# Keys and values of a second layer made in the experts' stage, and one accumulator for all experts

## The chip, the core and the metric

The kernel runs on one core of one Trainium2 chip, as one program. The core has five engines with a queue each: TensorE (matmuls; PE in the profile), VectorE (DVE), ScalarE (ACT), GpSimd (POOL) and SyncE (SP, which here only starts DMA transfers). They meet in semaphores alone. Sixteen DMA engines move data between DRAM and SBUF, the core's memory of 128 partitions; matmuls write to PSUM, eight banks of 512 f32 per partition. The metric is the device time in microseconds (us).

## The reference

64 sequences (NB) of 128 tokens with 256 features (D) go through two layers. `ctx` is one more input, a context for each sequence, the same in both layers.

```
x = x + tanh(g0) * attention0(layernorm(x), ctx, ctx)      # 16 heads of 16
x = x + tanh(h0) * experts(layernorm(x))                   # 64 experts, 8 for each token, at most 256 tokens each, and a shared one
x = x + tanh(g1) * attention1(layernorm(x), ctx, ctx, mask)
x = x + tanh(h1) * ffn(layernorm(x))                       # inner size 704, weights and activations rounded to 8 bits

attention(q, k, v) = softmax((q @ wq.T + bq) (k @ wk.T + bk).T / 4) (v @ wv.T + bv) @ wo.T + bo
expert e:  y[tokens of e] += gate[token, e] * (silu(x @ w1[e].T) * (x @ w3[e].T)) @ w2[e].T
```

The weights of the 8-bit FFN are scaled by the maximum of each row, rounded, and clipped.

## The kernel before, in words

The program has stages with a barrier of all engines behind each (`phase_end`).

Stage 2 is the first attention. Each engine runs through slots, one a sequence, and a function such as `values(k)` works on the sequence that its lag names (`attention_slots`, `stage(lag)`). A sequence's row of the residual stays in SBUF, in `res[:, b, :]`. At a slot's end `xa`, the residual with the shared expert's part added, is stored to the first accumulator in DRAM and zeros to the second; `token_rows` gets the normalised tokens with their gates. In the stage's last slots and behind them the weights of the 8-bit FFN are quantised: `weights_dve` on VectorE, `weights_pe` transposes, `weights_act` copies, and `ffn_weights_out` stores them to `ffn_int`. SyncE then loads the second layer's attention weights and the weights of the first experts.

Stage 3 is the experts', one slot an expert. GpSimd gathers 2 x 128 token rows two slots ahead (`gather`: two indirect DMAs, `xr<-token_rows`). TensorE transposes them (`rows_t`), multiplies by the first two weights (`up`, matmuls of 256 columns) and by the third (`down`). VectorE makes the hidden values and scales the outputs by the gate (`ye`). GpSimd adds them to an accumulator in DRAM (`add`: two indirect DMAs that accumulate). Expert b goes to accumulator b mod 2, and its add waits for the add of expert b - 2, since two adds at a time to one row would lose one. After the last expert TensorE and ScalarE make the keys and values of three sequences (`first_keys_values_pe`, `first_keys_values_act`).

Stage 4 is the second attention, slots again. SyncE loads the context and a row of both accumulators, VectorE adds the two into `res` (`first_sum`). TensorE, in each slot: `scores(m)` with the mask written first, `project_qk(f)`, `project_v(f)`, `scores_t(k)` with its mask, then transposes, `output`, `maxima_t` and `values`. `scores` and `scores_t` both write all of `tiles`, four banks of PSUM. VectorE's row maximum `mt` (L810) reads what `scores` wrote, and `scores_t`, of the sequence before, waits for it; ScalarE's exponential (L601) reads what `scores_t` wrote, and the next `scores` waits for that. Keys, and queries, are copied out of PSUM with their bias by ScalarE in `copy_qk`, values in `copy_v`.

Stages 5 and 6 are the 8-bit FFN, which the change leaves as it is. The order on each engine is the order in which the code issues; there is no scheduler.

Of the kernel before, what the change touches and what calls it, by code (L numbers as in the profile page):

```python
# [5 lines left out]
def flamingo_gated_two_layers(nc: bass.Bass, a, out: bass.AP):  # L6
# [44 lines left out]
    KV_FIRST = 3  # L51
# [3 lines left out]
    acc = [nc.dram_tensor(f"accumulator_{n}", [T + HALVES * P, D], f32).ap() for n in range(2)]  # L55
# [7 lines left out]
    hidden_away = nc.dram_tensor("hidden_away", [len(AWAY), P, IC * CT], f32).ap()  # L63
    ffn_int = nc.dram_tensor("ffn_int", [3, P, KC * IP], bf16).ap()

    ctx = ExitStack()
    with ctx:
# [146 lines left out]
        wraw = [qkp[:, 3 * n:3 * n + 3, :].rearrange("p a (c d) -> p (a c) d", d=D) for n in range(2)]  # L214
        wdraw = cxax[:, 0:6, :].rearrange("p a d -> p (a d)")[:, 0:KC * I].rearrange("p (k i) -> p k i", k=KC)
        wq_b = pt[1][:, 2:4, :].rearrange("p a d -> p (a d)").bitcast(bf16)[:, 0:KC * IP]
        ws = [w.rearrange("p a d -> p (a d)").bitcast(bf16)[:, 0:KC * IP] for w in (pt[0][:, 2:4, :], ovs[:, :, :], qkp[:, 0:2, :])]
# [78 lines left out]
        MADE_WEIGHTS = (8 if IREST else 6) * 2 + 11  # L296
# [26 lines left out]
        TILES_IN_0 = 8 * NB  # L323
# [3 lines left out]
        def attention_pe(pe, L):  # L327
            def sm(name):
                return f"{name}_{L}"

# [8 lines left out]
            def scores(m):  # L339
# [4 lines left out]
                wait(pe, sm("exp_done"), b - 1)  # L344
# [9 lines left out]
                last.then_inc(sem(sm("s_done")), 1)  # L354

            def scores_t(k):
# [4 lines left out]
                pe.wait_ge(sem(sm("max_done")), ahead(b, 2))  # L361
                if L == 1:
                    masks(1)
                pe.wait_ge(sem(sm("qm_done")), b + 1)
# [6 lines left out]
                last.then_inc(sem(sm("st_done")), 1)  # L371

            def maxima_t(m):
# [4 lines left out]
                pe.wait_ge(sem(sm("max_done")), b + 1)  # L378
# [6 lines left out]
                nc.tensor.transpose(bk[:, 0:P], mt[:, :], ident[:, :]).then_inc(sem(sm("mt_done")), 1)  # L385

            def values(k):
# [5 lines left out]
                pe.wait_ge(sem(sm("exp_done")), b + 1)  # L393
                pe.wait_ge(sem(sm("v_out")), b + 1)
                wait(pe, sm("at_out"), b)
# [5 lines left out]
                last.then_inc(sem(sm("pv_done")), 1)  # L401

            def transposes(f):
# [6 lines left out]
                if L == 0:  # L410
                    pe.wait_ge(sem(sm("v_out")), b + 1)
                else:
                    wait(pe, sm("v_out"), b)
# [4 lines left out]
            def project_qk(f):  # L418
# [5 lines left out]
                pe.wait_ge(sem(f"tile_in{r}"), (2 - L) * (4 * (b - r) + 16) + L * TILES_IN_0)  # L424
# [5 lines left out]
                for j in range(KC):  # L430
                    for n, w in enumerate((w_q, w_k)[:1 if L == 1 and b < KV_FIRST else 2]):
# [4 lines left out]
                last.then_inc(sem(sm("qk_done")), 1)  # L436

            def project_v(f):
                if f is None or (L == 1 and f[0] < KV_FIRST):
                    return  # L440
                b, r = f
                pe.wait_ge(sem(f"tile_in{r}"), (2 - L) * (4 * (b - r) + 16) + L * TILES_IN_0)
                if L == 0:
                    wait(pe, sm("silu_done"), b - 4)
                    wait(pe, sm("qm_done"), b - 1)
                else:
                    pe.wait_ge(sem(sm("xt_out")), b + 1)
# [3 lines left out]
                last.then_inc(sem(sm("v_done")), 1)  # L451

            def output(k):
# [4 lines left out]
                pe.wait_ge(sem(sm("at_out")), b + 1)  # L458
                if L == 0:
                    wait(pe, sm("x2t_out"), b)  # L460
                else:
                    pe.wait_ge(sem(sm("qm_done")), ahead(b, 3))
# [10 lines left out]
            def heads_to_tokens(k):  # L473
# [4 lines left out]
                pe.wait_ge(sem(sm("ov_out")), b + 1)  # L478
                for g in range(NG):
                    last = nc.tensor.transpose(bank[7][:, g * P:(g + 1) * P], ov[r % 2][:, g, :], ident[:, :])  # L480
                last.then_inc(sem(sm("ot_done")), 1)

            def tokens_to_heads(k):
# [4 lines left out]
                pe.wait_ge(sem(sm("on_done")), b + 1)  # L488
                for c in range(KC):
                    last = nc.tensor.transpose(bank[7][:, c * P:(c + 1) * P], on[r % 2][:, c * P:(c + 1) * P], ident[:, :])  # L490
                last.then_inc(sem(sm("at_done")), 1)
# [11 lines left out]
            def moe_up(k):  # L503
# [7 lines left out]
                pe.wait_ge(sem(sm("qm_done")), ahead(b, 4))  # L511
# [46 lines left out]
            def body(stage):  # L558
# [17 lines left out]
                else:  # L576
                    project_qk(f)
                    project_v(f)
# [11 lines left out]
        def attention_act(act, L):  # L590
            def sm(name):
                return f"{name}_{L}"
# [1371 lines left out]
        def _(dve):  # L1964
# [36 lines left out]
            for _ in ffn_weights:  # L2001
                pass
# [63 lines left out]
```

## Time and profile before

| | us |
|---|---|
| median of 3 runs | 2065.47 (2064.66 to 2066.73) |
| the profiled execution | 2067.25 |
| its span in the profile | 2065.4 |
| TensorE busy in the span | 1779.3 (86%) |
| VectorE busy | 1411.1 (68%) |
| ScalarE busy | 1108.9 (54%) |
| GpSimd busy | 562.2 (27%) |

Busy times are sums over stages with different limits, so they name no bound. A row of the timeline or the chain begins with its start in us and its length; `L1438` is line 1438 of the kernel; `accumulator<-ye,tid` is what is written and what is read. The chain of waits is followed back from the last instruction, at each step to what released it. For a DMA, its row in the timeline is the issuing; "to landing" is the time from the start of the issue until the data is there. TensorE's granted clock is 1.00 at 2.4 GHz and 0.50 at 1.2 GHz.

### The profile page before, as it was taken

How to read it: one execution, taken by the hardware profiler on the slowest of the kernel's cores; microseconds unless marked ns; L12 is line 12 of the kernel's file. 1: busy time of each engine (PE TensorE's matmuls, PEld its weight loads, DVE VectorE, ACT ScalarE, POOL GpSimd, SP SyncE). 2: the span in 40 equal slices, each digit the busy share in tenths (PEclk: the TensorE clock that was granted, in tenths of full speed). 3: DMA queues.
4: the chain of work that ended last, by engine and by line, in shares of the span. 5: the costliest groups of instructions: out<-in, count | busy, mean ns of one | idle time of the engine just before them, and what ended most of it. 6: DMA issues, size and time to landing. Idle time of an engine off the chain costs nothing.

```text
span 2065.4 us, 53950 instructions
## 1 busy us (share of the span) xinstructions
PE 1779.3 (86%) x20454; PEld 1404.9 (68%) x20464; DVE 1411.1 (68%) x4651; ACT 1108.9 (54%) x2283; POOL 562.2 (27%) x551
## 2 busy tenths in 40 slices
PE   6999999999999984677666667999999999978855
PEld 4888888888888873555555545777777777753334
DVE  4778788888878786544444425666666666657988
ACT  3666666666666641111111124666666666658875
POOL 1000000000000001788888871111111111111137
PEclk9999999999999995878878798999999999999989
DMA  3122221222222116667776752111111111102355
GB/s 98 49 67 63 66 64 61 72 63 66 63 67 63 61 48 192 151 151 150 146 151 151 152 96 62 48 47 42 48 40 48 41 48 44 37 25 100 145 201 207
DMA packets 158641, 180.49 MB, mean 87 GB/s; under 512 B 22512, under 2 KB 142704, under 8 KB 156208
## 3 DMA queue, kind: packets, MB, share of 16 engines
q1 hardware_dynamic: 133568, 138.41, 20.8%
q0 software_dynamic: 24816, 38.62, 10.3%
q8 instruction: 166, 2.72, 0.5%
q14 instruction: 91, 0.75, 0.1%
HBM read 108.85 MB, written 68.11 MB: 86 GB/s over the span
## 4 chain that ended last, share of the span: by engine, by line
PE 67%; DVE 16%; issue 6%; DMA 5%; POOL 4%; ACT 1%; POOLq 0%; SPq 0%; DVEq 0%; ACTq 0%
PE bank L434 12%; PE tiles L369 7%; PE tiles L352 7%; PE bank L399 6%; PE bank L517 6%; PE bank L449 5%; DMA xr<-token_rows,tid 4%; PE bank L480 4%; PE tiles L1252 3%; PE bank L469 3%; PE bank L540 3%; DVE hmax L1641 2%; PE tiles L336 2%; POOL accumulator L1438 2%; POOL xr L1423 2%
## 5 line engine op out<-in xcount | busy, mean ns | idle before, releaser
L1901 POOL TENSOR_TENSOR rstd<-var,minus_half 128x2 f32<-128x2 f32 x138 | 96.5, 699 | 1142.4 <-DVE var L887 1142.2
L810 DVE TENSOR_REDUCE mt<-tiles 128x16 f32<-128x2048 f32 x128 | 293.5, 2293 | 117.3 <-PE tiles L352 117.3
L601 ACT ACTIVATE pt<-tiles 128x2048 f32<-128x2048 f32 x128 | 240.8, 1881 | 13.2 <-PE tiles L369 8.6
L1438 POOL DMA_INDIRECT accumulator<-ye,tid x128 | 204.8, 1600 | 43.0 <-issue 29.0
L624 ACT ACTIVATE qkp<-bank,kb,keep 128x128 f32<-128x128 f32 x500 | 205.2, 475 | 0.0
L1386 DVE TENSOR_SCALAR ye<-bank,xr 128x256 f32<-128x256 f32 x128 | 56.0, 479 | 207.3 <-PE bank L1264 205.0
L1314 ACT COPY xrt<-tiles 128x512 f32<-128x512 f32 x64 | 37.5, 586 | 238.4 <-PE tiles L1234 238.4
L434 PE MATMUL bank<-xt,w_q 128*128 128x128 f32 x1024 | 164.4, 284 | 0.9 <-ACT xt L609 0.9
L1234 PE MATMUL tiles<-ident,xr 128*128 128x128 f32 x256 | 51.8, 336 | 129.8 <-DMA xr<-token_rows,tid 129.8
L621 ACT ACTIVATE qkp<-bank,qb 128x128 f32<-128x128 f32 x256 | 96.0, 376 | 123.5 <-PE bank L434 123.2
L1423 POOL DMA_INDIRECT xr<-token_rows,tid x128 | 137.1, 1071 | 79.7 <-DVE within L1354 42.1
L434 PE MATMUL bank<-cxax,w_k 128*128 128x128 f32 x1000 | 153.4, 276 | 0.0
L352 PE MATMUL tiles<-qkp 32*128 32x256 f32 x2048 | 149.0, 404 | 3.2 <-ACT qkp L624 3.2
L434 PEld LDWEIGHTS bank<-xt,w_q 128*128 128x128 f32 x1024 | 136.0, 194 | 22.9 <-issue 21.2
L369 PE MATMUL tiles<-qm,qkp 32*128 32x128 f32 x4096 | 150.3, 283 | 1.4 <-DVE mt L810 1.4
L369 PEld LDWEIGHTS tiles<-qm,qkp 32*128 32x128 f32 x4096 | 125.8, 186 | 27.2 <-issue 24.4
L399 PE MATMUL bank<-pt,vx 128*32 128x128 f32 x4096 | 139.1, 277 | 2.3 <-ACT pt L601 1.5
L469 PE MATMUL bank<-w_o,at 128*128 128x256 f32 x512 | 132.7, 382 | 0.5 <-ACT at L676 0.5
L434 PEld LDWEIGHTS bank<-cxax,w_k 128*128 128x128 f32 x1000 | 132.6, 193 | 0.0
L667 ACT COPY ovs<-bank 128x512 f32<-128x512 f32 x128 | 75.1, 587 | 102.7 <-PE bank L399 102.7
L449 PE MATMUL bank<-w_v,cxax 128*128 128x256 f32 x500 | 129.7, 382 | 0.0
L1234 PEld LDWEIGHTS tiles<-ident,xr 128*128 128x128 f32 x256 | 33.0, 165 | 141.1 <-DMA xr<-token_rows,tid 139.5
(251 smaller groups left out, 4004.1 us busy)
## 6 DMA issues: line engine op xcount, KB each, us to landing
cxax<-in_ctx SPq DMA_DIRECT2D x128, 128.0 KB, 2.2
cxax<-accumulator SPq DMA_DIRECT2D x128, 128.0 KB, 2.3
hidden_away<-h_ring SPq DMA_DIRECT2D x8, 1536.0 KB, 5.1
token_rows<-pay SPq DMA_DIRECT2D x64, 160.0 KB, 1.8
pt<-in_expert_up SPq DMA_DIRECT2D x36, 256.0 KB, 3.0
res<-in_x SPq DMA_DIRECT2D x64, 128.0 KB, 2.3
accumulator<-xa SPq DMA_DIRECT2D x64, 128.0 KB, 1.7
accumulator<-zt SPq DMA_DIRECT2D x64, 128.0 KB, 1.9
```

The lines of the kernel that those rows point to most:

```text
L352: last = nc.tensor.matmul(both, qt[r % 2][rows, j, :], kp[r][rows, :, j, :], start=(L == 0), stop=True, skip_group_check=(L == 1))
L369: last = nc.tensor.matmul(tiles[:, i, n * P:(n + 1) * P], kp[r][rows, e, j, :], qm[rows, e, j, :], start=(L == 0), stop=True, skip_group_c ...
L399: last = nc.tensor.matmul(bank[7][32 * h:32 * h + 32, g * P:(g + 1) * P], vx[r][:, GH * g + h, :], pt[p][:, i, n * P:(n + 1) * P], start=T ...
L434: last = nc.tensor.matmul(o_, w[:, c, j * P:(j + 1) * P], (cx[r] if n else xt[p])[:, c, :], start=(c == 0), stop=(c == KC - 1))
L449: last = nc.tensor.matmul(bank[4][:, 0:D], cx[r][:, c, :], w_v[:, c, :], start=(c == 0), stop=(c == KC - 1))
L469: last = nc.tensor.matmul(bank[6][:, 0:D], at[r % 2][:, c, :], w_o[:, c, :], start=(L == 1 and c == 0), stop=(c == KC - 1))
L517: last = nc.tensor.matmul(bank[4][:, n * FS + j * P:n * FS + (j + 1) * P], w[:, c, j * P:(j + 1) * P], x2t[p][:, c, :], start=(c == 0), st ...
L601: nc.scalar.activation(pt[r % 2][:, :, :], tiles[:, :, :], ACT.Exp).then_inc(sem(sm("exp_done")), 1)
L624: last = nc.scalar.activation(kp[r][:, e, j, :], bank[5][:, (KC + j) * P:(KC + j + 1) * P], ACT.Identity, bias=kb[:, e, j:j + 1], scale=ke ...
L810: nc.vector.tensor_reduce(mt[:, :].rearrange("p (i n c) -> p i n c", i=RT, n=2 * KC)[:, :, :, 0], tiles[:, :, :].rearrange("p i (n k) -> p ...
L1423: nc.gpsimd.indirect_dma_start(out=xr[n % ROWS_IN][:, h, :], out_offset=None, in_=rows[:, :], in_offset=bass.IndirectOffsetOnAxis(ap=tid[n ...
L1438: nc.gpsimd.indirect_dma_start(out=acc[p][:, :], out_offset=bass.IndirectOffsetOnAxis(ap=tid[b % 8][:, h:h + 1], axis=0), in_=ye[r][:, h, ...
```

## The change

- **Keys and values of the second layer in stage 3.** In each expert's slot TensorE runs `keys_or_values` between `rows_t` and `up`: four matmuls of 256 columns, in even slots the keys of two sequences, in odd slots their values. ScalarE copies the bank (`copy_pair`), SyncE stores it to `keys_values` in DRAM (`keep_pair`) and loads the contexts of a later pair (`load_pair`). In stage 4 SyncE loads a sequence's keys and values into `kvt`, and `copy_qk` and `copy_v` read them there instead of in PSUM. `project_qk` makes queries only, `project_v` is left out, and the work on the first three sequences at the end of stage 3 is gone.
- **One accumulator.** The store of zeros goes. Each add waits for the add of the expert before. In stage 4 SyncE loads the row straight into `res`; `first_sum` goes.
- **The FFN weights are quantised in stage 3.** They are loaded in slot 61 of stage 2, into the part of `res` (rows 8 to 55) that is free by then. VectorE does one step in most experts' slots; the transposes and copies come in slots 8 and 9, 13 and 14, 20 and 21 (`WEIGHTS_AT`), the stores in slots 11, 16 and 23. Each weight has a buffer of its own.
- Semaphores that counted each layer apart now count both in one (`first = L * NB`), with the same waits.

```diff
@@ experts_pool, add
-                wait(pool, f"e_added{p}", 16 * (b - p))
+                wait(pool, f"e_added{1 - p}", 16 * (b + p))
                 for h in range(HALVES):
                     nc.gpsimd.indirect_dma_start(
-                        out=acc[p][:, :], out_offset=bass.IndirectOffsetOnAxis(ap=tid[b % 8][:, h:h + 1], axis=0),
+                        out=acc[:, :], out_offset=bass.IndirectOffsetOnAxis(ap=tid[b % 8][:, h:h + 1], axis=0),
@@ experts_pe
+            def keys_or_values(e):
...
+                pe.wait_ge(sem(f"pair_in{j % 4}"), 8 * (j - j % 4) + 32)
+                wait(pe, "kv_out", n)
+                for k in range(2):
+                    for c in range(KC):
+                        if n % 2 == 0:
+                            weights_, moving = w_k[:, c, k * P:(k + 1) * P], cxp[j % 4][:, c, :, :].rearrange("p e t -> p (e t)")
+                        else:
+                            weights_, moving = cxp[j % 4][:, c, k, :], w_v[:, c, :]
+                        last = nc.tensor.matmul(bank[5][:, k * D:(k + 1) * D], weights_, moving, start=(c == 0), stop=(c == KC - 1))
+                last.then_inc(sem("kv_done"), 1)
...
                 rows_t(stage(0))
+                keys_or_values(stage(0))
                 up(stage(1))
                 down(stage(2))
-                if stage(0) is not None and stage(0)[0] == E // 4 + 10:
+                if stage(0) is not None and stage(0)[0] in WEIGHTS_AT:
+                    next(weights, None)
@@ experts_act
+                nc.scalar.copy(kvs[p], bank[5][:, :]).then_inc(sem("kv_out"), 1)
@@ experts_sp
+                sp.wait_ge(sem("kv_out"), n + 1)
+                sp.dma_start(keys_values[n], kvs[p]).then_inc(sem(f"kv_kept{p}"), 16)
+                if p == 1 and n // 2 + 4 < PAIRS:
+                    load_pair(sp, n // 2 + 4)
@@ experts_dve
+                if stage(0) is not None and stage(0)[0] > 2 and stage(0)[0] != E // 4 and stage(0)[0] != E // 4 + 4:
+                    next(weights, None)
@@ attention_pe, L == 1
-                    for n, w in enumerate((w_q, w_k)[:1 if L == 1 and b < KV_FIRST else 2]):
+                    for n, w in enumerate((w_q, w_k)[:2 - L]):
...
                     project_qk(f)
-                    project_v(f)
                     scores_t(k)
@@ attention_act, copy_qk
+                if L == 1:
+                    act.wait_ge(sem(f"kv_in{p}"), 16 * (b - p) + 32)
...
+                    k = bank[5][:, (KC + j) * P:(KC + j + 1) * P] if L == 0 else kvt[p][:, j * P:(j + 1) * P]
@@ attention_sp
-                        sp.dma_start(ax[p][:, n_, :], acc[n_][bass.ds(b * P, P), :]).then_inc(sem(f"ax_in{p}"), 16)
+                sp.dma_start(row(b), acc[bass.ds(b * P, P), :]).then_inc(sem(f"row_in{p}"), 16)
...
-                sp.dma_start(acc[1][bass.ds(b * P, P), :], zt[:, 0, 0:D]).then_inc(sem("acc_zero"), 16)
@@ the end of stage 2
             first_expert_weights(sp)
-            ffn_weights_out(sp)
...
-            weights_act(act)
...
-            weights_pe(pe)
...
-            for _ in ffn_weights:
-                pass
```

GpSimd in stage 3, before, from the first expert's add (`ye0`) on; in brackets the semaphores that an instruction waits for, where `e_added0` counts the adds of even experts and `e_added1` those of odd ones:

```order
L1438 DMA accumulator_0<-ye0,tid0 8448x256 [waits e_y_done]
L1438 DMA accumulator_0<-ye0,tid0 8448x256
L1423 DMA xr0<-token_rows,tid5 128x320 [waits e_y_done,e_t_done,e_slot_step]
L1423 DMA xr0<-token_rows,tid5 128x320
L1438 DMA accumulator_1<-ye1,tid1 8448x256 [waits e_y_done]
```

The same place in the changed kernel:

```order
L1477 DMA accumulator<-ye0,tid0 8448x256 [waits e_y_done]
L1477 DMA accumulator<-ye0,tid0 8448x256
L1462 DMA xr0<-token_rows,tid5 128x320 [waits e_y_done,e_t_done,e_slot_step]
L1462 DMA xr0<-token_rows,tid5 128x320
L1477 DMA accumulator<-ye1,tid1 8448x256 [waits e_added0,e_y_done]
```

No instruction moved; the second expert's add waits for the first one's, and so on for each expert.

TensorE in stage 4, before, from the masks ahead of `scores` (L352) to the transposes of the heads (L480):

```order
L336 MATMUL tiles<-mask_bias,identb 32x512 x16
L352 MATMUL tiles<-qkp 128x2x128 x8
L434 MATMUL bank<-xt,w_q 128x128 x2
L434 MATMUL bank<-cxax,w_k 128x128 x2
L434 MATMUL bank<-xt,w_q 128x128 x2
L434 MATMUL bank<-cxax,w_k 128x128 x2
L449 MATMUL bank<-w_v,cxax 128x256 x2
L336 MATMUL tiles<-mask_bias,identb 32x512 x16
L369 MATMUL tiles<-qm,qkp 128x128 x16
L480 MATMUL bank<-ident,ovs 128x128 x4
```

The same place in the changed kernel (`scores` is L361, `scores_t` L378):

```order
L345 MATMUL tiles<-mask_bias,identb 32x512 x16
L361 MATMUL tiles<-qkp 128x2x128 x8
L444 MATMUL bank<-xt,w_q 128x128 x4
L345 MATMUL tiles<-mask_bias,identb 32x512 x16
L378 MATMUL tiles<-qm,qkp 128x128 x16
L487 MATMUL bank<-ident,ovs 128x128 x4
```

Between the two groups that write `tiles` only the queries are left. What came from here stands in stage 3, in the slot of an expert (odd and then even, `L1268`), with the transposes (L1282) ahead of it, and `up` (L1300) and `down` (L1312) behind:

```order
L1282 MATMUL tiles<-ident,xr 128x128 x4
L1268 MATMUL bank<-w_v,res 128x256 x4
L1300 MATMUL tiles<-xrt,pt 128x256 x4
L1312 MATMUL bank<-wlast,ht 128x256 x2
L1543 MATMUL tiles<-identb,res 128x128 x6
L1249 MATMUL bank<-table,begun 128x130 x2
```

The row of L1543 is one half of an FFN weight's transposes, in slot 8 or 9.

## Rows read from the trace of the kernel before

**Rows 1.** Stretches: length, busy us by engine (instructions), granted clock, DMA share, GB/s.

```profile
828.00:1224.00 396.00, 269.13 (x1101) 207.99 (x1100) 176.88 (x746) 59.47 (x123) 322.21 (x240) 0.83 0.70 147
1268.00:1838.00 570.00, 557.20 (x8899) 420.47 (x8891) 379.90 (x844) 383.45 (x789) 85.74 (x121) 1.00 0.15 44
2000.00:2020.00 20.00, 11.59 (x100) 9.18 (x98) 19.55 (x32) 18.00 (x29) 16.15 (x18) 1.00 1.02 405
```

**Rows 2.** Timeline of GpSimd's adds, one expert: start, length, instruction, idle before.

```profile
1019.49 1.62 POOL L1438 DMA_INDIRECT accumulator<-ye,tid  x1 [0.30 <-issue]
1021.42 1.58 POOL L1438 DMA_INDIRECT accumulator<-ye,tid  x1 [0.30 <-DVE ye L1386]
...
1026.07 1.62 POOL L1438 DMA_INDIRECT accumulator<-ye,tid  x1 [0.30 <-issue]
```

**Rows 3.** Chain of waits, one turn of the second attention: start, length, what.

```profile
1508.10 0.36 PE tiles L336 x16
...
1509.54 1.98 PE bank L434 x16
1511.52 0.87 PE bank L449 x4
1512.38 0.36 PE tiles L336 x16
...
1513.85 0.60 PE bank L480 x4
```

**Rows 4.** Timeline of the same turn: the maximum, and the next turn's masks.

```profile
1509.61 2.29 DVE L810 TENSOR_REDUCE mt<-tiles 128x16 f32<-128x2048 f32 x1 [1.04 <-PE tiles L352]
...
1517.30 0.43 PE L336 MATMUL tiles<-mask_bias,identb 32*32 32x512 bf16 x16
```

**Rows 5.** Timeline at the end of the first attention, SyncE and TensorE.

```profile
790.45 0.48 SPq L1144 DMA_DIRECT2D table<-table_rows  x1
...
800.18 0.43 SPq L1181 DMA_DIRECT2D xt<-in_L_ffn_w  x1
...
807.77 0.22 PE L1209 MATMUL bank<-table,halves_tri 128*128 128x32 bf16 x1 [1.17 <-SPq L257]
```

**Rows 6.** Timeline of TensorE, two groups of `up` in the first experts' slots.

```profile
819.49 3.62 PE L1252 MATMUL tiles<-xrt,wlast 128*128 128x256 f32 x8
...
824.28 1.89 PE L1252 MATMUL tiles<-xrt,pt 128*128 128x256 f32 x8
```

**Rows 7.** Chain of waits at the first expert's add.

```profile
827.07 0.89 DVE ye L1386 x2
...
828.78 0.37 POOL accumulator L1438
```

**Rows 8.** Single adds by line: the first, the last, and the longest one's landing.

```profile
L1438 POOL DMA_INDIRECT accumulator<-ye,tid x1: 1582/1582/1582, 863.6 to 863.6; - x1
L1438 POOL DMA_INDIRECT accumulator<-ye,tid x1: 1582/1582/1582, 1218.6 to 1218.6; - x1
DMA to landing us min/median/max: 5.6/5.6/5.6
```

**Rows 9.** DMA queues from 860 to 1230: packets, MB, share of 16 engines.

```profile
q1 hardware_dynamic: 15504, 20.45, 18.8%
```

**Rows 10.** Timeline at the mask step, then groups by line from 771 to 808.

```profile
914.23 1.69 POOL L1438 DMA_INDIRECT accumulator<-ye,tid  x1 [0.30 <-issue]
914.98 0.85 DVE L1830 TENSOR_SCALAR mask_bias<-res 128x1024 bf16<-128x1024 int32 x1
...
L769 DVE TENSOR_TENSOR qkp<-qkp,inv 128x1536 f32<-128x1536 f32 x2 | 3.5, 1754 | 0.0
...
L771 DVE TENSOR_SCALAR qkp<-qkp 128x1536 f32<-128x1536 f32 x2 | 1.9, 959 | 0.1
```

**Rows 11.** Timeline of GpSimd, the last two halves.

```profile
1231.70 1.56 POOL L1438 DMA_INDIRECT accumulator<-ye,tid  x1 [0.30 <-issue]
1233.57 1.56 POOL L1438 DMA_INDIRECT accumulator<-ye,tid  x1 [0.30 <-issue]
```

More of the change, by code:

```diff
@@ L329, in sm @@
                 return f"{name}_{L}"
+            first = L * NB
             def masks(n):
@@ L343, in scores @@
                 b, r = m
-                wait(pe, sm("exp_done"), b - 1)
+                wait(pe, "exp_done", first + b - 1)
                 if L == 1:
@@ L461, in output @@
                 else:
-                    pe.wait_ge(sem(sm("qm_done")), ahead(b, 3))
+                    pe.wait_ge(sem("qm_done"), first + ahead(b, 3))
                     wait(pe, sm("x3_done"), b)
@@ L510, in moe_up @@
                 pe.wait_ge(sem(sm("xt_out")), ahead(b, 5))
-                pe.wait_ge(sem(sm("qm_done")), ahead(b, 4))
+                pe.wait_ge(sem("qm_done"), first + ahead(b, 4))
                 if b == 0:
@@ L756, in weights_dve @@
                 dve.wait_ge(sem("w_int"), 1)
-            yield
-            st = once(dve, "weights")
             for n in range(2):
@@ L794, in weights_dve @@
-            st.then(V.tensor_copy(at[0][:, :, :], s_d[:, :].unsqueeze(2).broadcast_to([P, KC, P])))
+            st.mark(V.reciprocal(sig[:, :], sig[:, :]))
+            st.mark(V.tensor_copy(at[0][:, :, :], s_d[:, :].unsqueeze(2).broadcast_to([P, KC, P])))
+            yield
+            for _ in range(5):
+                yield
             dve.wait_ge(sem("sd_t"), 1)
-            st.then(V.tensor_copy(sd_row[:, :], bank[1][:, 0:D]))
+            st.mark(V.tensor_copy(sd_row[:, :], bank[1][:, 0:D]))
@@ L1045, in body @@
                     routing(1)
-                    if v is not None and v[0] == NB - 1:
-                        next(ahead_of_time)
                     routing(1)
@@ L1082, in body @@
                     gate_scales()
-                if L == 0 and v is not None:
-                    for _ in range({NB - 3: 1, NB - 2: 1, NB - 1: 3}.get(v[0], 0)):
-                        next(ahead_of_time)
             attention_slots(body, FIRST[L])
@@ L1147, in body @@
             def body(stage):
-                load(stage(-2 if L == 0 else -3))
-                if L == 0:
-                    if stage(5) is not None and stage(5)[0] == NB - 2:
+                if L == 1:
+                    load_keys_values(stage(-1))
+                    load_sums(stage(-3))
+                else:
+                    load(stage(-2))
+                    if stage(5) is not None and stage(5)[0] == ROOM_TO:
                         ffn_weights_in(sp)
@@ L1322, in gate_tanh, with copy_pair @@
                 nc.scalar.activation(sg[r % 2][:, :], bank[2 + r % 2][:, 0:CAP], ACT.Tanh, scale=0.5).then_inc(sem("e_sg_done"), 1)
+            def copy_pair(e):
+                if e is None:
+                    return
+                n, r = e
+                p = r % 2
+                act.wait_ge(sem("kv_done"), n + 1)
+                wait(act, f"kv_kept{p}", 8 * (n - p))
+                nc.scalar.copy(kvs[p], bank[5][:, :]).then_inc(sem("kv_out"), 1)
             def body(stage):
                 copy_t(stage(0))
+                copy_pair(stage(0))
                 gate_tanh(stage(1))
+                if stage(0) is not None and stage(0)[0] in WEIGHTS_AT:
+                    next(weights, None)
+            weights = weights_act(act)
             expert_slots(body)
@@ L1793, in value_bias_out @@
             for c in range(KC):
-                last = nc.tensor.matmul(bank[6 - L][:, 0:D], at[0][:, c, :], w_o[:, c, :], start=(c == 0), stop=(c == KC - 1))
+                last = nc.tensor.matmul(bank[(6, 1)[L]][:, 0:D], at[0][:, c, :], w_o[:, c, :], start=(c == 0), stop=(c == KC - 1))
             last.then_inc(sem("bv_out"), 1)
```

338 lines of the change are left out of this document (172 added, 166 removed).

## The prediction

> **What bounds the kernel now.** I read the stretches first, then the page of busy times, then the chain of waits and the timeline inside each stretch. The changed parts are the tail of the first attention, the experts (808 to 1242 us), and the second attention, of which 1268 to 1838 is the even part [rows 1]. Each has a limit of its own, so each is read alone.
>
> In the experts' stage GpSimd sets the pace. One expert is a first half of an add at 1019.49, a second at 1021.42, two gathers, and the next add at 1026.07 [rows 2]. Each instruction starts 0.30 us after the end of the one before, which is the number in square brackets, and none waits for data. The period is 1026.07 - 1019.49 = 6.58 us; four issues and four gaps fill it. The other engines have room: TensorE is busy 269 of 396 us, VectorE 177, ScalarE 59 [rows 1].
>
> In the second attention one score buffer (`tiles`) goes round: masks and scores, row maximum, masks and scores again, exponential. [rows 3] is one turn of the chain of waits from 1508.10; the next turn's masks start at 1517.30 [rows 4], so it takes 9.2 to 9.3 us. TensorE is busy 557 of 570 us there, but the reader should see that it shares the turn with VectorE's maximum.
>
> **The tail of the first attention.** The FFN weights are quantised there now, and the stage's barrier falls at 807.77, behind their last store [rows 5]. With this work gone, what is late next is SyncE's own queue: the order keeps twenty loads (attention weights, first experts) behind the table load of 790.45, and the last of them, at 800.18, ends at 800.6. With the same 0.4 us from the last issue's end to the first matmul as now, the experts start at 801.0. **Gain 7 us.** Of the moved steps, 13 issues of 0.4 to 0.5 us go to SyncE's slot 61, ahead of that slot's stores, which nobody awaits for two slots: nothing.
>
> **The experts' start.** TensorE gets four matmuls of 256 columns per expert, the shape and number of `up`, which took 1.89 us at full clock and 3.62 at half [rows 6]. They stand between the transposes and `up`, and three such groups come before the first add: 5.7 us at full clock, 10.9 at half. Part of that lies in the waits for the first gathers, and `up` then finds the clock risen. **Cost 5 us** (0 to 11).
>
> **The experts' period.** What decides is the new wait. Before, add b waited for add b-2; now it waits for add b-1. From a release to the start of such a DMA GpSimd's queue needs 828.78 - 827.96 = 0.8 us [rows 7]: register moves, hidden today beside the instruction that runs. The next add starts 4.65 us after the second half of the last (1026.07 - 1021.42). A landing after more than 4.65 - 0.84 = 3.8 us therefore delays it, and everything behind it on GpSimd: its second half, both gathers, and by these TensorE. I read the landing of each of the 55 second halves from 863.6 to 1218.6 by itself (first, last and the longest in [rows 8]): mean 4.09 us, 13 of them 4.5 or more, and a mean excess over 3.8 of 0.30 us. At today's traffic the change costs 0.30 us an expert.
>
> The traffic grows. SyncE loads 384 KB an expert now; 128 KB of context and 256 KB of keys or values are added, which doubles it. The 16 DMA engines are 0.70 busy [rows 1]; at the price that SyncE's packets pay (18.8% for 20.45 MB over 370 us [rows 9]), 25.2 MB more add 0.21. Most landings are 3.8 or 3.9, so I take the long ones for those that meet a burst of SyncE's: twice the bursts, twice the excess, 0.61 us. Ends: 0.12 (only what exceeds 4.35 us, if the 0.8 us stayed hidden) and 1.3 (landings of 5.1 as a rule). I take 0.61, for 59 adds with gathers between. **Cost 36 us** (7 to 77).
>
> The Trainium skill (DMA: Bandwidth & Descriptors, "Latency and other measured facts") puts an HBM access at 0.2 us on average and 2 us at high load. By that figure, an estimate, a landing could grow by 1.8 us and this term reach 106 us. The trace agrees in direction only, with a longest landing of 5.6 [rows 8].
>
> The other additions hide. ScalarE's copies and VectorE's weight steps of up to 1.75 us [rows 10] find engines that are idle most of each 6.58 us. TensorE's share grows by 1.9 us an expert; from a gather to the add of the same slot lie two periods, 13 us, and today TensorE still waits for gathers inside them. At half clock (3.6 us) that cover would be nearly gone, and the sign would be GpSimd waiting for `ye`.
>
> The Trainium skill (SBUF — State Buffer, "Who interferes with whom") says that a VectorE instruction in a two-port mode locks GpSimd out, so that its DMA descriptors aren't written, and that one with two SBUF inputs delays GpSimd's reads. In this trace an add that ran beside a `mask_bias` step of 0.85 us took 1.69 us [rows 10], an ordinary one 1.62 [rows 2]: 0.07 more. By the rule the seven moved steps of these kinds (four or more of 0.96 us, three of 1.75 or less) would cost GpSimd up to 10.7 us; by the row well under 1.
>
> **The experts' end.** After the last gather four experts' adds follow back to back, each half 1.87 us after the other [rows 11]. Now the first half of each must wait for a landing: 3.8 + 0.84 = 4.64 instead of 1.87. 4 x 2.77 = **cost 11 us** (9 with the 0.8 hidden).
>
> **The second attention.** `w_k` and `w_v` go: half of 1.98 us and all of 0.87, together 1.86 us of TensorE per tile [rows 3]. They stand between the scores and the second masks. But the second masks need the maximum, which runs from 1509.61 for 2.29 us, to 1511.90 [rows 4], and they start at 1512.38 now. So there are 0.48 us to win, less about 0.05 for TensorE's release. What is late next is VectorE's maximum, and TensorE idles 1.4 us. From the second scores' end to the next masks 3.45 us pass, which hold no removed instruction. **Gain 0.43 x 61 tiles = 26 us** (23 to 28). ScalarE's copies of keys and values read SBUF instead of PSUM, but start a microsecond earlier, beside the maximum; two loads a tile ahead take the place of three, at a DMA share of 0.15. The VectorE sum that goes lay in idle time: nothing.
>
> **Sum.** -7 + 5 + 36 + 11 - 26 = +19 us, on the profiled execution's 2067.25: 2086. That execution lies 1.8 us above the median of the runs, so I expect 2084.
>
> **Rivals.** (1) *The landings stay hidden*: the 0.8 us is overlapped as now and traffic does nothing. -7 + 5 + 7 + 9 - 26 = -12, or 2053; 2048 if the start is free too. For it: most landings are 3.8. Against: the queue's work behind a wait [rows 7]. (2) *Today's excess and no more*, 0.30 x 59 = 18 us: -7 + 5 + 18 + 11 - 26 = +1, 2066. (3) *TensorE bounds the second attention*, busy 557 of 570 as it is. Then 1.86 x 61 = 113 us go instead of 26: 1997. Against: the maximum's 2.29 us in the same turn, past which the second masks can't go. (4) *The DMA engines saturate*: 0.70 + 0.21 leaves little, and landings of 5.1 give 77 instead of 36: 2125. It decides once half the landings exceed 4.6. (5) *The port lock in full*: 2084 + 10 = 2094. (6) *The clock falls* in the second attention with 1.4 us idle per tile: two groups of masks and scores (1.44 + 1.47 us [rows 3]) double, over 100 us. Against: from 2000 to 2020 TensorE is busy 58% and granted 1.00 [rows 1]. (7) *The change does not do what it says*, because keys from DRAM come late: no 26 us, 2110.
>
> **How the numbers follow.** Forecast 0.44, (1) 0.22, (2) 0.12, (3) 0.03, (4) 0.11, (5) 0.04, (6) 0.02, (7) 0.02. About 0.2%, 4 us, is what can be told from no change. Of (2) half lies within it and a quarter on each side; the forecast's own range, 2070 to 2105, touches it. So faster 0.29, same 0.09, slower 0.62. The range for eight in ten goes from 2049, which takes in (1), to 2116.
>
> **What would show it.** Right: GpSimd's adds with a wait for `DMA accumulator`, a period near 7.2 us, landings of 4.4 on average, experts from 801, a turn of 8.8 us in the second attention with TensorE waiting for `mt`. Wrong: adds that still start 0.30 us after a gather in most experts, or a turn far from 8.8.

## The result, and the profile after

| | us |
|---|---|
| before, median of 4 runs | 2065.06 (2060.92 to 2066.73) |
| after, median of 4 runs | 2086.66 (2085.17 to 2088.01) |
| ratio | 1.0107 (1.009 to 1.0125) |
| the profiled execution after, its span | 2086.53, 2084.8 |

The change makes the kernel 1% slower, 2086.7 where 2084 was forecast. I cut both profiled executions at the same events and subtracted: the first and last start of VectorE's maximum in each attention, TensorE's first matmul behind the barrier, GpSimd's adds.

| stretch, us | before | after | difference | forecast |
|---|---|---|---|---|
| start to the last maximum of the first attention | 744.87 | 742.56 | -2.3 | 0 |
| from there to the barrier | 62.90 | 53.43 | -9.5 | -7 |
| barrier to the first add | 21.01 | 24.13 | +3.1 | +5 |
| 59 experts' periods | 387.92 | 427.41 | +39.5 | +36 |
| start of expert 59's add to the last half's start | 16.87 | 27.77 | +10.9 | +11 |
| from there to the second attention's first maximum | 20.60 | 19.69 | -0.9 | 0 |
| its first to its last maximum | 580.20 | 556.52 | -23.7 | -26 |
| from there to the end | 231.03 | 233.29 | +2.3 | 0 |

The first and the last line are no effect: in the ten profiles of this study the last maximum of the first attention starts between 742.6 and 748.9, and the end takes 228 to 233.

The experts' stage first. Timeline of GpSimd in the changed kernel: start, length, instruction, idle before it and what ended it ([rows 2] before).

```profile
1197.87 1.62 POOL L1477 DMA_INDIRECT accumulator<-ye,tid  x1 [1.24 <-DMA accumulator<-ye,tid]
1199.79 1.59 POOL L1477 DMA_INDIRECT accumulator<-ye,tid  x1 [0.30 <-issue]
1201.68 1.09 POOL L1462 DMA_INDIRECT xr<-token_rows,tid  x1 [0.30 <-issue]
1203.09 1.05 POOL L1462 DMA_INDIRECT xr<-token_rows,tid  x1 [0.31 <-issue]
1205.19 1.62 POOL L1477 DMA_INDIRECT accumulator<-ye,tid  x1 [1.06 <-DMA accumulator<-ye,tid]
```

The four instructions are as long as before; new is the idle time of 1.24 and 1.06 us ahead of the first half, which the landing of the expert before ends. The chain of waits over the same expert shows what the queue adds ([rows 7] before):

```profile
1199.79 4.55 DMA accumulator<-ye,tid
...
1204.45 0.52 issue
...
1205.00 0.20 issue
...
1205.19 0.38 POOL accumulator L1477
```

The second half lands after 4.55 us, and the next add starts 5.40 us after it: 0.85 us for the register moves between, where [rows 7] had 0.82. Over 58 experts the second halves had a mean landing of 4.41 us and a mean excess over 3.8 us of 0.63 (before 4.09 and 0.31), from single adds read as in [rows 8]. The line's summary, and one long landing:

```profile
DMA to landing us min/median/max: 3.5/4.1/6.2
...
L1477 POOL DMA_INDIRECT accumulator<-ye,tid x1: 1589/1589/1589, 1083.8 to 1083.8; - x1
...
DMA to landing us min/median/max: 5.5/5.5/5.5
```

What SyncE issued around that add, from its timeline: contexts 1.0 us ahead, expert weights 0.8 us behind.

```profile
1082.80 1.00 SPq L1529 DMA_DIRECT2D res<-in_ctx  x2
1084.64 0.34 SPq L1195 DMA_DIRECT2D pt<-in_expert_up  x1
1085.03 0.43 SPq L1196 DMA_DIRECT2D xn<-in_L_ffn_w  x1
```

SyncE's queue from 860 to 1230 ([rows 9] before), and the stretches ([rows 1] before): length, busy us by engine, granted clock, DMA share, GB/s.

```profile
q1 hardware_dynamic: 35232, 40.51, 34.5%
...
828.00:1224.00 396.00, 320.61 (x1463) 259.88 (x1462) 179.08 (x724) 89.63 (x170) 294.92 (x219) 0.90 0.81 193
...
1300.00:1860.00 560.00, 463.18 (x8283) 335.69 (x8281) 359.60 (x797) 401.18 (x802) 87.16 (x123) 0.99 0.15 47
```

The bytes doubled (20.45 to 40.51 MB), and GpSimd, the stage's bound, is busy for 295 us of 396 instead of 322, because it waits. The last adds, from its timeline ([rows 11] before), each behind the landing of the one before:

```profile
1254.09 1.57 POOL L1477 DMA_INDIRECT accumulator<-ye,tid  x1 [3.06 <-DMA accumulator<-ye,tid]
1255.96 1.56 POOL L1477 DMA_INDIRECT accumulator<-ye,tid  x1 [0.30 <-issue]
1260.55 1.56 POOL L1477 DMA_INDIRECT accumulator<-ye,tid  x1 [3.03 <-DMA accumulator<-ye,tid]
```

The barrier: SyncE's last load and TensorE's first matmul ([rows 5] before). Then the keys' first two groups, at half and at full clock, from the chain of waits.

```profile
795.18 0.43 SPq L1196 DMA_DIRECT2D xt<-in_L_ffn_w  x1
795.99 0.22 PE L1237 MATMUL bank<-table,halves_tri 128*128 128x32 bf16 x1 [13.70 <-SPq L265]
...
805.38 3.41 PE bank L1268 x8
...
809.71 1.81 PE bank L1268 x8
```

The second attention, one turn in the chain of waits ([rows 3] before), and the same second masks in the timeline ([rows 4] before):

```profile
1519.15 1.01 PE bank L408 x32
1520.16 0.36 PE tiles L345 x16
1520.52 1.12 PE tiles L361 x16
...
1521.67 2.31 DVE mt L825
...
1524.02 0.44 PE tiles L345 x16
...
1529.07 0.36 PE tiles L345 x16
...
1524.02 0.44 PE L345 MATMUL tiles<-mask_bias,identb 32*32 32x512 bf16 x16 [1.33 <-DVE mt L825]
```

The queries have left the chain and the maximum has entered it. TensorE waits 1.33 us for it here, and in every turn from 1400 to 1800 (us in total, times, longest):

```profile
PE tiles L345 <- DVE mt L825: 58.4, 44, 1.3
```

The turn, from the first masks of one to those of the next, is 1529.07 - 1520.16 = 8.91 us. Before it was 9.27, from 1508.10 [rows 3] to this row of the chain:

```profile
1517.37 0.36 PE tiles L336 x16
```

### The profile page after: what moved, and what is told of

Same layout as the page of the kernel before. It is cut to its first block, busy times and chain, and to the rows that moved or that the text cites. A ratio compares the mean times of both kernels' runs of the same rounds, so it can differ in the third digit from the quotient of the medians.

```text
span 2084.8 us, 53641 instructions
## 1 busy us (share of the span) xinstructions
PE 1753.1 (84%) x20198; PEld 1386.3 (66%) x20208; DVE 1382.9 (66%) x4585; ACT 1156.6 (55%) x2347; POOL 563.3 (27%) x550
## 4 chain that ended last, share of the span: by engine, by line
PE 57%; DVE 19%; issue 7%; DMA 7%; POOL 6%; ACT 1%; SPq 1%; POOLq 1%; DVEq 0%; ACTq 0%
DVE mt L825 8%; PE tiles L378 7%; PE tiles L361 7%; PE bank L408 6%; PE bank L444 6%; PE bank L524 5%; DMA accumulator<-ye,tid 4%; PE bank L487 4%; POOL accumulator L1477 3%; PE bank L476 3%; PE bank L547 3%; PE bank L456 3%; DMA xr<-token_rows,tid 3%; PE tiles L345 2%; DVE hmax L1690 2%
## 5 line engine op out<-in xcount | busy, mean ns | idle before, releaser
L444 PE MATMUL bank<-xt,w_q 128*128 128x128 f32 x1024 | 153.3, 283 | 0.9 <-ACT xt L616 0.9
L378 PE MATMUL tiles<-qm,qkp 32*128 32x128 f32 x4096 | 151.1, 284 | 1.4 <-DVE mt L825 1.4
L361 PE MATMUL tiles<-qkp 32*128 32x256 f32 x2048 | 148.0, 401 | 3.5 <-ACT qkp L633 3.4
L444 PEld LDWEIGHTS bank<-xt,w_q 128*128 128x128 f32 x1024 | 130.2, 192 | 22.6 <-issue 20.2
L378 PEld LDWEIGHTS tiles<-qm,qkp 32*128 32x128 f32 x4096 | 126.6, 187 | 27.5 <-issue 24.6
L345 PE MATMUL tiles<-mask_bias,identb 32*32 32x512 bf16 x2048 | 56.3, 388 | 84.7 <-DVE mt L825 84.7
L1282 PE MATMUL tiles<-ident,xr 128*128 128x128 f32 x256 | 46.6, 310 | 84.8 <-DMA xr<-token_rows,tid 84.8
L361 PEld LDWEIGHTS tiles<-qkp 32*128 32x128 f32 x2048 | 92.3, 184 | 35.3 <-issue 26.9
L915 DVE RECIPROCAL rden<-bank 128x16 f32<-128x16 f32 x128 | 32.4, 253 | 124.3 <-PE bank L487 124.3
L837 DVE SCALAR_TENSOR_TENSOR qm<-bank,keep,qkp 128x256 f32<-128x256 f32 x256 | 111.0, 475 | 5.2 <-PE bank L394 4.9
L408 PEld LDWEIGHTS bank<-pt,vx 128*32 128x32 f32 x4096 | 104.1, 109 | 15.1 <-ACT pt L608 3.0
```

Of the source, the lines that this page charges most:

```text
L345: nc.tensor.matmul(tiles[32 * j:32 * j + 32, i, :], identb[rows, rows], mask_bias[rows, n, j, :].unsqueeze(1).broadcast_to([32, 2 * KC, S] ...
L361: last = nc.tensor.matmul(both, qt[r % 2][rows, j, :], kp[r][rows, :, j, :], start=(L == 0), stop=True, skip_group_check=(L == 1))
L378: last = nc.tensor.matmul(tiles[:, i, n * P:(n + 1) * P], kp[r][rows, e, j, :], qm[rows, e, j, :], start=(L == 0), stop=True, skip_group_c ...
L408: last = nc.tensor.matmul(bank[7][32 * h:32 * h + 32, g * P:(g + 1) * P], vx[r][:, GH * g + h, :], pt[p][:, i, n * P:(n + 1) * P], start=T ...
L444: last = nc.tensor.matmul(o_, w[:, c, j * P:(j + 1) * P], (cx[r] if n else xt[p])[:, c, :], start=(c == 0), stop=(c == KC - 1))
L837: last = nc.vector.scalar_tensor_tensor(qm[:, e, :, :], bank[4 if L == 0 else 6][:, 0:P].unsqueeze(1).broadcast_to([P, KC, P]), keep[:, 1 ...
```

## The experiments

Four kernels ran against the same runs of before in each of two groups; a ratio is always to before. Cut as above, from one profile each:

| us | before | after | e1 | e2 | e3 | e4 | e5 | e6 | e7 | e8 |
|---|---|---|---|---|---|---|---|---|---|---|
| last maximum to barrier | 62.9 | 53.4 | 54.0 | 62.9 | 53.8 | 53.7 | 52.4 | 52.3 | 52.0 | 63.3 |
| barrier to first add | 21.0 | 24.1 | 24.6 | 21.0 | 24.2 | 24.1 | 23.6 | 23.5 | 23.7 | 24.2 |
| 59 periods | 387.9 | 427.4 | 390.7 | 400.8 | 405.3 | 406.5 | 427.4 | 413.5 | 426.4 | 425.3 |
| last adds | 16.9 | 27.8 | 18.0 | 27.9 | 27.9 | 27.9 | 28.7 | 28.6 | 28.7 | 27.8 |
| second attention | 580.2 | 556.5 | 556.7 | 578.9 | 557.3 | 556.6 | 557.4 | 557.4 | 516.6 | 556.5 |

**e1, two accumulators again, all else as changed.**

```diff
-                wait(pool, f"e_added{1 - p}", 16 * (b + p))
+                wait(pool, f"e_added{p}", 16 * (b - p))
...
+                sp.dma_start(acc[1][bass.ds(b * P, P), :], zt[:, 0, 0:D]).then_inc(sem("acc_zero"), 16)
...
-                sp.dma_start(row(b), acc[bass.ds(b * P, P), :]).then_inc(sem(f"row_in{p}"), 16)
+                for n_ in range(2):
+                    sp.dma_start(ax[p][:, n_, :], acc[n_][bass.ds(b * P, P), :]).then_inc(sem(f"ax_in{p}"), 16)
...
+                nc.vector.tensor_tensor(row(b), ax[p][:, 0, :], ax[p][:, 1, :], ALU.add).then_inc(sem(sm("sum_done")), 1)
```

> The changed kernel with the two accumulators of before: zeros stored to the second one, an add waits for the add of expert b-2, both rows loaded in stage 4 and added on VectorE. My theory: the whole loss lies in the wait for the previous add, so the experts' period falls from 7.24 to the 6.58 us that GpSimd's four DMAs take (59 x 0.66 = 39 us less) and the four adds behind the last gather follow 1.87 us apart again (11 us less), although SyncE's traffic stays doubled; the sum in stage 4 lies in VectorE's idle time. 2087 - 39 - 11 = 2037 us, 28 below the kernel before. Rival, keys and values themselves slow the experts' stage (TensorE or the DMA engines bind): a period over 6.9, 2055 or more. Rival, the 0.4 us of the sum lengthens the turn of the second attention: 2037 + 25 = 2062.

Measured: 2044.78 us (2041.84 to 2053.49), ratio 0.9912 (0.9896 to 0.9928): **faster than both kernels**. The stretches of its experts (length, busy, clock, DMA share, GB/s), and two first halves of adds:

```profile
828.00:1208.00 380.00, 318.62 (x1543) 260.23 (x1542) 188.06 (x750) 95.01 (x180) 309.68 (x230) 0.95 0.88 209
...
1010.85 1.62 POOL L1488 DMA_INDIRECT accumulator<-ye,tid  x1 [0.30 <-DMA accumulator<-ye,tid]
...
1017.42 1.62 POOL L1488 DMA_INDIRECT accumulator<-ye,tid  x1 [0.30 <-DMA accumulator<-ye,tid]
```

At the same bytes per expert, and so at a higher share (0.88) and 209 GB/s, GpSimd starts again 0.30 us after each instruction. The period is 6.62 us: keys, values and traffic cost the stage 2.8 us in all, against 39.5 with the wait. In 55 of 58 experts SyncE issues something within 1.5 us of the second half, and it costs nothing, since nobody waits for that landing. The sum on VectorE leaves the second attention at 556.7. Against after the periods give 36.7 and the last adds 9.7, where I had expected 39 and 11. The profiled execution took 2041.84 us, 4.8 more than the expected 2037, of which these two make 3.6; the median of the runs lies another 2.9 above it. Both rivals fall: the period is under 6.9, and the sum costs the second attention 0.2 us.

**e2, the kernel before with serial adds only.**

```diff
-                wait(pool, f"e_added{p}", 16 * (b - p))
+                wait(pool, f"e_added{1 - p}", 16 * (b + p))
```

> The kernel before, with one line changed: each add waits for the add of expert b-1 instead of b-2; both accumulators are kept and keys, values and weights stay where they were. My theory: at the traffic of before the mean excess of a landing over 3.8 us is 0.31, so 59 x 0.31 = 18 us, and 11 us behind the last gather: 2065 + 29 = 2094, mean landing 4.1. Rival, a serial add costs the same at any traffic (the wait itself brings the loads and the adds into step): 59 x 0.66 = 39 and 11, 2115. Rival, the waits find gaps again: 2076.

Measured: 2088.51 us (2086.03 to 2092.77), ratio 1.0122 (1.0108 to 1.0137). One line costs 24 us, more than the whole change nets. Periods +12.9, last adds +11.0. The mean excess was 0.20 us, not 0.31. The second halves' mean landing fell from 4.09 to 3.98 us while the first halves' rose from 4.11 to 4.17; that the shifted adds met the loads elsewhere is my reading, which no run tests. My 29 was 5 too high; both rivals fall.

**e3, the changed kernel without the stores of keys and values and without the contexts** (all but the first pair, and the first four pairs).

```diff
-                sp.dma_start(keys_values[n], kvs[p]).then_inc(sem(f"kv_kept{p}"), 16)
-                if p == 1 and n // 2 + 4 < PAIRS:
-                    load_pair(sp, n // 2 + 4)
+                if n < 2:
+                    sp.dma_start(keys_values[n], kvs[p]).then_inc(sem(f"kv_kept{p}"), 16)
```

> The changed kernel; SyncE stores keys and values of the first pair only and loads the contexts of the first four pairs only, and stage 4 reads that first pair again and again, so its output is another one. TensorE's, ScalarE's and GpSimd's instructions and all waits between them stay. My theory: SyncE's doubled traffic lengthens the landings of the adds; without it the mean landing goes back from 4.41 to 4.1, the period from 7.24 to 6.9, and the time from 2087 by 59 x 0.31 = 18 to 2068. Rival, the longer landings come from adding to one accumulator or from the adds' own rhythm: 2087 as before, landings 4.4.

Measured: 2070.81 us (2069.67 to 2073.88), ratio 1.0032 (1.0021 to 1.0042). SyncE's queue from 860 to 1230, then the line's landings:

```profile
q1 hardware_dynamic: 15408, 21.63, 19.9%
...
DMA to landing us min/median/max: 3.7/3.9/5.5
```

The mean landing is 4.06 us and the period 6.87, so the periods are 22 us shorter than after, while all of TensorE's added work stayed. The expected 2068 was 3 too low, and the rival falls. So 22 of the 39.5 us come from the added traffic, and e2 gives 12.9 to the wait at the old traffic. Of the 4.6 that are left for the added work of the engines, 3.9 stand in GpSimd's own DMA instructions: from the first to the 60th add they sum to 319.5 us here and to 315.6 in e2 (315.9 before). The last section shows what lengthens them.

**e4, the changed kernel with SyncE held back** until the first half of an add has landed, and **e5, its control** with the two semaphores but no hold.

```diff
+                sp.wait_ge(sem(f"e_early{x % 2}"), 8 * (x - x % 2) + 16)      # e4 only; x is the slot's number less 4
...
-                wait(pool, f"e_added{1 - p}", 16 * (b + p))
+                for name in ("e_early", "e_added"):
+                    wait(pool, f"{name}{1 - p}", 8 * (b + p))
```

> The changed kernel with SyncE's loads and stores of stage 3 held back, slot by slot, until the first half of an add has landed (the halves count in semaphores of their own for that), so that they are issued from 1.9 us after the start of a second half on and are through before the next second half. All bytes are moved as before. My theory: what lengthens a landing is a load or store issued within about 1.4 us ahead of the add or 1.5 us behind it; moved away from the second halves, their landings are 3.8 to 3.9 nearly always, the period is 6.65 to 6.75 and the time 2087 - 59 x 0.53 = 2055. Rival, it is the amount of traffic and not the moment: 2087, landings 4.4. Rival, the held loads come too late for TensorE or ScalarE: over 2087, with TensorE waiting for expert weights.

> The changed kernel, whose adds count their two halves in two semaphores each, as in the run with held-back loads, and so wait for two semaphores instead of one; SyncE is not held back. It is the control for that run, which came out at 2067 where I expected 2055, with 0.92 to 0.98 us from a landing to the next add instead of 0.86. My theory: the second wait costs 0.1 us an expert, 59 x 0.1 = 6 us: 2093, with landings of 4.4 on average; the gain from the moment of the loads alone is then 26 us. Rival, the second semaphore costs nothing: 2087. Rival, it was the second semaphore and not the held-back loads that shortened the landings: 2067.

Measured: e4 2066.72 us (2058.66 to 2073.35), ratio 1.001 (0.9996 to 1.0023); e5 2088.10 us (2083.91 to 2091.02), ratio 1.0105 (1.0091 to 1.0119). The second semaphore costs nothing, so the hold gains 21 us, 20.9 of them in the periods, at unchanged bytes. GpSimd's waits for landings from 860 to 1200 in e5 and in e4: us in total, times, longest.

```profile
POOL accumulator L1480 <- DMA accumulator<-ye,tid: 19.1, 13, 1.9
POOL accumulator L1480 <- DVE ye L1424: 12.3, 9, 2.5
```

```profile
POOL accumulator L1487 <- DMA accumulator<-ye,tid: 9.5, 7, 1.8
```

The second row of e5 puts waits down to VectorE's `ye`, but in the seven long ones that `ye` ended only 0.03 to 0.39 us ahead of the add, less than the 0.85 us that a release takes. I count them as waits for landings, as the landings in the profile of after explain such waits there. Then 31.4 us stand against 9.5, which is about the gain.

And SyncE in one slot of e4: all five are issued 2.7 us or more behind the second half of 1008.11, and the last two run into the next first half, of 1013.02, whose landing does not decide.

```profile
1010.85 0.33 SPq L1195 DMA_DIRECT2D qm<-in_expert_up  x1
1011.22 0.44 SPq L1196 DMA_DIRECT2D xt<-in_L_ffn_w  x1
1011.70 0.43 SPq L1220 DMA_DIRECT2D keys_values<-res  x1
1012.18 1.05 SPq L1540 DMA_DIRECT2D res<-in_ctx  x2
```

The profile of e4 has the landings of the even experts' second halves and of the odd experts' first halves alone (29 each). The second halves have a mean of 3.90 us, where the same ones in after have 4.52; the first halves' rose from 4.09 to 4.88. That is the forecast mechanism, shown for every other expert. The other second halves are seen only through the start of the next add: 5.07 us after them on average, against 5.19 in after, so most of the gain lies with the even experts. TensorE waits for no expert weights from 860 to 1200, only for gathers, so the rival of loads that come too late falls; the rival of the amount falls with the time.

But the period stayed at 6.89, not 6.7. In ten experts the next add started over 5.35 us after a second half, and in nine of these SyncE issued nothing within 1.5 us of it. Four of the ten have a GpSimd instruction that VectorE's quantisation lengthened, three of them (ahead of experts 3, 8 and 12) a gather, with no wait for a landing at all. The one ahead of expert 8, from the timelines of VectorE and GpSimd (1.09 us is usual for this gather):

```profile
876.92 1.75 DVE L777 TENSOR_TENSOR res<-res,inv 128x1536 f32<-128x1536 f32 x1
877.34 2.30 POOL L1471 DMA_INDIRECT xr<-token_rows,tid  x1 [0.30 <-issue]
```

In the other six the landing was long, up to 5.04 us where it is known; what made it long stays open. It is not the 0.1 us for the semaphore that I had put into e5's expectation: e5's periods equal after's, and in e4 the add starts 0.88 us after the landing, not 0.92 to 0.98.

**e6, the changed kernel with SyncE held back until the whole add has landed.**

> The changed kernel with SyncE held back, slot by slot, until both halves of an add have landed (no second semaphore). Its first load is then issued 0.8 us ahead of the next first half, 2.7 us ahead of the next second half; in a slot with contexts the last of five is issued near 1 us ahead of the second half. My theory (the moment decides): the second halves of every other slot are spared, mean landing 4.1, period 6.9 to 7.0, 2087 - 59 x 0.3 = 2069. Rival, any hold helps by the whole: 2055. Rival, the amount of traffic decides: 2087.

Measured: 2074.16 us (2072.61 to 2079.75), ratio 1.005 (1.0037 to 1.0063); period 7.01. It lies between e4 and after, as the moment would have it, 5 us above the expected 2069; that any hold helps by the whole is wrong, and so is that the amount alone decides.

**e7, the changed kernel with a maximum over every second score in the second attention.**

```diff
-                                        tiles[:, :, :].rearrange("p i (n k) -> p i n k", n=2 * KC),
+                                        tiles[:, :, :].rearrange("p i (n k) -> p i n k", n=2 * KC)[:, :, :, 0:P:L + 1],
```

> The changed kernel; in the second attention VectorE's maximum reads every second score only, so the output is another one. My theory: the turn of 8.92 us runs over this maximum of 2.29 us, during which TensorE waits 1.33 us; at 1.15 us (if a strided read is no slower per element) the turn falls by 1.15 to 7.77, until TensorE's own queries stand in the way, and the time by 61 x 1.15 = 70 us to 2017. Rival, TensorE's work or ScalarE's exponential binds the turn, and the maximum lies beside it: 2087, or less than 20 us below. Rival, a strided read takes the 2.29 us all the same: no change, with the duration showing it.

Measured: 2043.24 us (2041.21 to 2052.24), ratio 0.9908 (0.9888 to 0.9928). From its timeline, VectorE's maximum and the second masks behind it, then the chain's exponential:

```profile
1546.71 1.23 DVE L825 TENSOR_REDUCE mt<-tiles 128x16 f32<-128x1024 f32 x1 [1.47 <-PE tiles L361]
...
1547.99 0.44 PE L345 MATMUL tiles<-mask_bias,identb 32*32 32x512 bf16 x16 [0.26 <-DVE mt L825]
...
1548.04 0.86 ACT qkp L633 x2
...
1549.83 0.39 ACT vx L647
1550.22 1.21 ACT pt L608
```

The maximum is 1.06 us shorter and the turn 0.65 (8.27), 40 us over the attention: the maximum did bind. But 0.5 us above my 7.77 ScalarE takes over, so the time fell by 43 us and not by 70: its copies of queries, keys and values stand ahead of the exponential and are the chain now. I had named only TensorE's queries as the next bound.

**e8, the FFN weights quantised ahead of the barrier again**, the rest as changed.

```diff
             attention_dve(dve, 0)
+            dve.wait_ge(sem("o_done_0"), NB)
+            for _ in weights_dve(dve):
+                pass
```

> The changed kernel with the FFN weights quantised at the end of the first attention again (loads in slot 61 as in the changed kernel, all VectorE, TensorE and ScalarE steps and the three stores ahead of the stage's barrier); keys, values and one accumulator as in the changed kernel. My theory: from the last maximum of the first attention to the barrier 53.4 us become some 63, as in the kernel before, and GpSimd's DMA instructions, which lost 2 us to VectorE's long steps in stage 3, gain them back: 2087 + 9 - 2 = 2094. Rival, the quantisation costs more in stage 3 than it saves, because it also delays TensorE and VectorE ahead of the first adds: 2085 or less.

Measured: 2092.13 us (2090.05 to 2093.87), ratio 1.0133 (1.0118 to 1.0148). The barrier is 9.8 us later, the periods give 2.1 back, and the rival (2085 or less) falls. The first add comes no sooner after the barrier (24.2), so the quantisation is not what costs the 3 us there; of the additions the keys' and values' work is left, whose matmul groups stand in the chain above (3.41 and 1.81 us).

## Why the prediction was right, and where its steps were not

**The new wait decides: right.** e1 takes it away and everything returns, e2 adds it alone and loses 24 us. The size, 36 us for the periods, came within 4 of 39.5, and its inputs were met: 0.85 us from landing to start (0.84 in the sum, 0.82 by [rows 7]), mean excess 0.63 (forecast 0.61).

**How the traffic works: half right.** I had taken twice the bursts for twice the excess. I sorted 116 halves in each profile by whether SyncE issued anything from 1.4 us ahead of their start to 1.5 behind. Before, 70 had such an issue, with a mean landing of 4.25, and 46 had none, 3.88. After, 81 had one, 4.65, and 35 none, 3.89. So there are not twice as many meetings; each is worse. That it is because a slot now issues up to five DMAs in a row is my guess, which no run separates. And e2 and e3 put the excess at the old traffic at 0.20 and 0.27, not at 0.30 (0.31 here, over 58 halves): a smaller base met a larger factor, and that their product came out right was luck. The Trainium skill (DMA: Bandwidth & Descriptors, "Latency and other measured facts") lets an HBM access grow from 0.2 to 2 us at high load; the trace agrees in so far as single landings reach 6.2. But in e4, at 205 GB/s from 860 to 1200, the second halves that were kept clear of the loads still land after 3.90 us on average: the amount alone does not make them long.

**The experts' start, +5:** 3.1 measured, inside the forecast's 0 to 11. The keys' first group ran at half clock (3.41 us) and the next at full clock (1.81).

**The experts' end, +11: right** (10.9, and 11.0 in e2). Of the two prices, 9 with the 0.8 us hidden fell: idle times of 3.03 and 3.06 us stand ahead of these adds.

**The barrier, -7: direction right, 2.5 us too small.** The queue behind the table load was as forecast: last issue's end 795.61, first matmul 795.99. What I had missed is that the table load itself came 2.6 us sooner after the last maximum. One group of matmuls, which ran at a granted clock of 0.50 and now runs at 1.00, makes 0.9 of it; before, then after:

```profile
780.43 2.07 PE L540 MATMUL bank<-w_sd,ht 128*128 128x256 f32 x4 [1.15 <-DVE ht L938]
```

```profile
777.21 1.13 PE L547 MATMUL bank<-w_sd,ht 128*128 128x256 f32 x4 [1.26 <-DVE ht L944]
```

Three more groups ahead of it in the chain are together 0.9 shorter, and 0.6 goes with VectorE's quantisation steps that stood among its routing steps. e8, which has the quantisation behind the last output, keeps this part: its table load comes 43.2 us after the last maximum, against 45.6 before and 43.0 after.

**The second attention, -26: the step "past the maximum it can't go" was right** (e7), the size 2.3 us too large. From the first masks to the second it is now 1524.02 - 1520.16 = 3.86 us, against 4.28 [rows 3]: the forecast 0.43, all but 0.01. The other half of the turn gives 0.06 back, 1529.07 - 1524.02 = 5.05 against 1517.37 - 1512.38 [rows 3] = 4.99. The second masks take 0.44 us of the chain where they took 0.36 [rows 3]: in the timelines the group is 0.43 to 0.44 us long both times, but before it began beside the end of the values' matmuls, and now it starts from an idle engine. I had left that out.

**The rivals.** Hidden landings and today's excess fall with the 35.8 us that GpSimd waits for landings between the first and the 60th add (1.2 before). TensorE bounding the second attention falls with its 1.33 us of waiting. The DMA engines did not saturate: e1 moves the same bytes per expert faster. In the second attention the clock stayed at 0.99. Keys came in time: nothing in the chain of the second attention waits for them. The port lock in full (10 us) falls, but a part of it is real and my "well under 1" was wrong: GpSimd's 256 DMA instructions sum to 344.1 us, 341.9 before, and e8 gets 2.1 us of the periods back by moving VectorE's steps away. The row that I had judged by misled me: that `mask_bias` step began 0.75 us after the add [rows 10], and those that cost began before the GpSimd instruction.

## What to carry to other kernels

Before two buffers that take turns are merged, read how long the landing takes that the second one hid, and compare it with what the issuing engine has between two uses, its register work included; here 3.8 us of landing and 0.85 of release stood against 4.65, with no margin at all. Once such a wait exists, transfers that another queue issues near it can cost time, and then shifting them is worth about as much as taking them away: the periods fell by 20.9 us in e4, which moved all bytes, and by 22.1 in e3, which left the added ones out. Neither comes near a second accumulator (36.7 in e1). And take a bundle apart: two of three parts gained here (9 and 24 us, for 6 us of their own cost), and the third cost 46 (36.7 and 9.7 against e1).

## What the runs showed of the hardware

In these traces a GpSimd instruction that issues an indirect DMA grows by a little less than what is left of a long VectorE instruction on SBUF that began before it. From the timelines of VectorE and GpSimd, after, then e3:

```profile
873.05 1.75 DVE L777 TENSOR_TENSOR res<-res,inv 128x1536 f32<-128x1536 f32 x1
873.83 2.44 POOL L1477 DMA_INDIRECT accumulator<-ye,tid  x1 [0.30 <-issue]
```

```profile
842.80 1.75 DVE L777 TENSOR_TENSOR res<-res,inv 128x1536 f32<-128x1536 f32 x1
842.94 3.06 POOL L1476 DMA_INDIRECT accumulator<-ye,tid  x1 [0.30 <-PE tiles L1281]
```

Both are second halves of adds, which usually take 1.58 us; 0.97 us of the VectorE instruction were left in the first case and 1.61 in the second, and the add took 0.9 and 1.5 us more. A `TENSOR_SCALAR` of 0.95 us does the same on its scale (an add of 2.24 us in e6, where it began 0.17 us ahead). The Trainium skill (SBUF — State Buffer, "Who interferes with whom") has the lock for `tensor_scalar` in its two-port modes. For `tensor_tensor` with both inputs in SBUF it says that it contends with GpSimd's reads, and it infers that descriptor generation is spared. Here the issue of the DMA is late all the same; whether it is the read of the row numbers (`tid`) or the descriptors that waits, no run separates. The quantisation has nine such steps in the stage, three `TENSOR_TENSOR` and six `TENSOR_SCALAR`, and what they cost depends on where they fall: GpSimd's 256 instructions sum to 2.2 us more than before in after, and 6.0 more in e4.
